# A two-layer block on one core: the first half of x2 is formed during the scan, the work behind the scan is reordered, and the first decay and delta times u go ahead of x's high parts and remainders

## The chip, the core and the metric

The kernel runs on one core of a Trainium2 chip. The core has TensorE (PE), VectorE (DVE), ScalarE (ACT), GpSimd (POOL), SyncE (SP, which issues most transfers) and 16 DMA engines. Each engine works through its own queue in order, and the engines wait for one another on semaphores. The metric is the device time of one execution in microseconds; lower is better.

## The reference, cut to what matters

`x` is (4, 256, 256), `ctx` is (4, 256, 128), so there are 1024 tokens of 256 channels.

```python
x = x + tanh(g_xattn[0]) * attention(layernorm(x), ctx, ...)               # x1
x = x + tanh(g_ffn[0])   * ffn(layernorm(x), w_gate_up, w_proj)            # x2
x = x + tanh(g_xattn[1]) * ssm(ctx, z=layernorm(x), ...)                   # x3
x = x + tanh(g_ffn[1])   * moe(layernorm(x), router, gate, up, down)       # result

# ffn, both weight matrices quantised to three values per group of 64
h = silu(x @ gate.T) * (x @ up.T)
hn = h * rsqrt(mean(h * h) + eps)
return hn @ w_proj.T

# ssm: 16 states n for each of 256 channels e, 256 time steps, 4 batches
state = state * exp(delta * A) + (delta * u) * B
y = sum_over_n(state * C) + D * u
return y * silu(z)

# moe: 64 experts, 8 per token, 128 slots per expert
logits = x @ router; top 8; gather, two matmuls, silu, one matmul, scatter
```

## The kernel before, in words

Every engine has its program written out by hand, one function per engine, and nothing reorders it.

**Up to the scan.** Attention, convolution, `delta`, the quantisation of the feed-forward weights and the normalisation of x1 are done. PE turns the normalised rows into banks 1 to 4 (`transpose_tokens(2, ...)`), one bank per pair of channel half and token half. ACT's `keep_high(k)` (L831) copies bank 1 + k into `x_high` at a shorter mantissa, and DVE (L1543) subtracts that from the bank into `x_low`, the remainder, so that two matmuls stand for one of full precision. ACT's `keep_quantised(k)` (L824) copies the turned ternary weights out of banks 5, 6, 7 and 0. DVE multiplies `delta` by `u` into bank 5 (L1548), once bank 5 has been read.

**The scan.** 64 steps k (4 phases of 16 states; a step covers 512 tokens). Per step ACT's `decay(k)` (L861) writes exp(delta A) into one of three buffers `dA`; DVE's `state(k)` multiplies bank 5 by the row B (L1565, into bank 6 or 4 in turn) and runs the recurrence (L1570) into one of four buffers `hs`. Two steps make one POOL `product` (L612) with C, which PE turns and sums into bank 3 (L1104). A DVE step that reuses a buffer of `hs` waits for the product that read it two pairs before. The step's unit f = k // 4 also carries one of 16 slices of the feed-forward block: PE's `gate_up(f)` (L1162), ACT's silu (L898, with a load of its table before and one back for the exponential), the gate times up on DVE (`hidden`, L1578) or, for every fourth f, on POOL, its square (ACT L881, POOL L626) and PE's `project` (L1135). At f = 8 the projection of the first four token tiles is complete and ACT copies it to `xn` (L874); at f = 10 POOL forms their root of mean squares (`rms(0)`, L631).

**Behind the scan.** DVE forms the last product (L1627), the mean squares of the second half (L1554), coefficient and x2 of tiles 0 to 3 (L1602, L1608), their statistics (L1614, L1617), then the same for tiles 4 to 7, three small tables from `ident` (L1636 to L1639, used far later, by the routing), and y times silu(z) (`gated`, L1645). ACT keeps the last y (`keep_y(3)`, L868), the turned x2 (`keep_x2`, L917) and silu of the normalised x2 (`gate_z`, L923). PE turns x2 (L1206) and y (L1258), and computes the router's logits of x2 (L1225) and of y (L1233). Then come the choice of 8 experts (`select`), the list of slots, and the loop over 64 experts, which ends the program.

## Time and profile before

| | us |
|---|---|
| median of 3 runs (lowest, highest) | 399.18 (398.72, 400.62) |
| the profiled execution, its own time | 399.68 |
| its span, first to last instruction | 397.9 |
| up to the scan | 0 to 62.3 |
| start of the scan and scan | 62.3 to 194.0 |
| behind the scan, up to the second half of the logits | 194.0 to 211.7 |
| choice and slots, up to the first expert's rows | 211.7 to 229.3 |
| expert loop and end | 229.3 to 397.9 |
| PE busy, DVE busy, ACT busy, POOL busy (share of the span) | 328.9 (83%), 303.7 (76%), 257.6 (65%), 247.4 (62%) |

All times in the sections below count from the start of the span. A busy time is that of the engine's own instructions; a row of a timeline gives the start, the length, the engine, the line, what is written from what, and in brackets how long the engine sat idle before it and for whom. The length of a DVE or ACT instruction includes some 0.1 us in which the next one already runs.

### The profile page before, as it was taken

How to read it: one execution, taken by the hardware profiler on the slowest of the kernel's cores; microseconds unless marked ns; L12 is line 12 of the kernel's file. 1: busy time of each engine (PE TensorE's matmuls, PEld its weight loads, DVE VectorE, ACT ScalarE, POOL GpSimd, SP SyncE). 2: the span in 40 equal slices, each digit the busy share in tenths (PEclk: the TensorE clock that was granted, in tenths of full speed). 3: DMA queues.
4: the chain of work that ended last, by engine and by line, in shares of the span. 5: the costliest groups of instructions: out<-in, count | busy, mean ns of one | idle time of the engine just before them, and what ended most of it. 6: DMA issues, size and time to landing. Idle time of an engine off the chain costs nothing.

```text
span 397.9 us, 6795 instructions
## 1 busy us (share of the span) xinstructions
PE 328.9 (83%) x1854; PEld 270.4 (68%) x1857; DVE 303.7 (76%) x669; ACT 257.6 (65%) x528; POOL 247.4 (62%) x194
## 2 busy tenths in 40 slices
PE   3947964887797699598885189999999999999994
PEld 2433643575585578487685177888888888888863
DVE  2999999999999999999999946554544455544485
ACT  1798999998888898888264345445544554445412
POOL 4200025779887778797423488888787888787410
PEclk9996885799999989989999579999999999999999
DMA  8940620776344887341297348888898888874464
GB/s 232 366 155 2 172 80 26 246 265 222 115 151 165 272 259 262 109 158 54 61 263 187 115 108 219 213 216 225 223 225 233 229 223 221 212 156 94 67 189 144
DMA packets 57835, 70.96 MB, mean 178 GB/s; under 512 B 6659, under 2 KB 42163, under 8 KB 57811
## 3 DMA queue, kind: packets, MB, share of 16 engines
q1 hardware_dynamic: 49104, 56.04, 46.0%
q0 software_dynamic: 7536, 14.56, 15.9%
q10 hardware_dynamic: 1170, 0.08, 0.2%
q8 instruction: 11, 0.18, 0.2%
q14 instruction: 14, 0.11, 0.1%
HBM read 61.75 MB, written 8.91 MB: 178 GB/s over the span
## 4 chain that ended last, share of the span: by engine, by line
PE 43%; DVE 15%; ACT 10%; DMA 7%; issue 7%; POOL 1%; DVEq 0%; SPq 0%; POOLq 0%
PE bank L1326 14%; PE bank L1349 11%; PE bank L1319 7%; DVE bank L1565 5%; DMA ssm<-bc_rows 4%; PE bank L1306 4%; DVE ssm L1570 3%; ACT ssm L861 3%; DMA B_last<-bc_rows 2%; ACT L898 2%; PE bank L1312 2%; ACT L861 1%; ACT ffn L898 1%; PE bank L1162 1%; PE bank L1233 1%
## 5 line engine op out<-in xcount | busy, mean ns | idle before, releaser
L612 POOL TENSOR_TENSOR ssm<-ssm,arena 128x1024 f32<-128x1024 f32 x31 | 73.7, 2376 | 19.5 <-DVE ssm L1570 11.4
L683 POOL DMA_INDIRECT ssm<-routed,idx x64 | 67.7, 1058 | 21.8 <-issue 18.6
L1570 DVE TENSOR_TENSOR_SCAN ssm<-ssm,bank 128x512 f32<-128x512 f32 x64 | 78.1, 1221 | 2.2
L1326 PE MATMUL bank<-places,ye_parts 128*128 128x512 f32 x264 | 75.8, 412 | 0.5 <-DVE ye_parts L1782 0.5
L1790 DVE SCALAR_TENSOR_TENSOR ssm<-ssm,bank 128x96 f32<-128x96 f32 x64 | 20.1, 314 | 71.8 <-ACT ssm L970 71.7
L694 POOL DMA_INDIRECT sums<-ssm,idx x31 | 52.9, 1706 | 14.4 <-issue 9.4
L970 ACT ACTIVATE ssm<-bank 128x96 f32<-128x96 f32 x64 | 16.0, 250 | 69.9 <-PE bank L1349 69.9
L1349 PE MATMUL bank<-arena,ssm 128*128 (+1 forms) x256 | 53.3, 330 | 1.1 <-ACT ssm L953 1.1
L1326 PEld LDWEIGHTS bank<-places,ye_parts 128*128 128x128 f32 x264 | 45.3, 189 | 12.1 <-DVE ye_parts L1782 0.9
L1349 PEld LDWEIGHTS bank<-arena,ssm 128*128 128x128 f32 x256 | 45.1, 191 | 7.2 <-issue 1.7
L861 ACT ACTIVATE ssm<-delta,A_sb 128x510 f32<-128x510 f32 x64 | 44.1, 716 | 7.8 <-DVE ssm L1570 7.5
L1104 PE MATMUL bank<-ident,ssm 128*128 128x128 f32 x256 | 34.4, 280 | 16.4 <-ACT bc_buf L868 8.4
L580 POOL TENSOR_TENSOR rstd<-rstd,mhalf 128x4 f32<-128x4 f32 x8 | 9.2, 1154 | 62.0 <-DVE rstd L1414 61.9
L1104 PEld LDWEIGHTS bank<-ident,ssm 128*128 128x128 f32 x256 | 29.5, 144 | 21.2 <-POOL ssm L612 10.1
L1319 PE MATMUL bank<-arena,ssm 96*128 (+1 forms) x128 | 38.7, 384 | 0.5 <-ACT ssm L957 0.5
L1565 DVE TENSOR_TENSOR bank<-bank,ssm 128x512 f32<-128x512 f32 x44 | 29.9, 679 | 0.1
L953 ACT ACTIVATE ssm<-bank 128x256 f32<-128x256 f32 x64 | 24.5, 383 | 7.5 <-PE bank L1306 7.5
L1306 PE MATMUL bank<-ident,ssm 128*128 128x128 f32 x128 | 25.5, 282 | 4.4 <-DMA ssm<-routed,idx 4.4
L963 ACT ACTIVATE ssm<-bank 128x256 f32<-128x256 f32 x64 | 24.6, 384 | 6.5 <-PE bank L1319 3.6
L1774 DVE TENSOR_SCALAR places<-xin,fix 128x1024 fp32r<-128x1024 f16 x33 | 25.7, 780 | 0.5 <-PE bank L1326 0.4
L1306 PEld LDWEIGHTS bank<-ident,ssm 128*128 128x128 f32 x128 | 23.0, 198 | 4.5 <-DMA ssm<-routed,idx 4.4
L1162 PE MATMUL bank<-x_high,w_gate 128*128 128x512 f32 x32 | 16.0, 501 | 8.8 <-ACT w_up L824 3.3
(232 smaller groups left out, 698.4 us busy)
## 6 DMA issues: line engine op xcount, KB each, us to landing
ssm<-bc_rows SPq DMA_DIRECT2D x22, 512.0 KB, 3.8
arena<-bc_rows SPq DMA_DIRECT2D x16, 512.0 KB, 5.0
arena<-in_L_ffn_gate_proj SPq DMA_DIRECT2D x32, 192.0 KB
arena<-in_L_ffn_up_proj SPq DMA_DIRECT2D x32, 192.0 KB
arena<-in_L_ffn_down_proj SPq DMA_DIRECT2D x32, 192.0 KB
B_last<-bc_rows SPq DMA_DIRECT2D x10, 512.0 KB, 3.8
sums<-zero_f SPq DMA_DIRECT2D x1, 2304.0 KB, 14.1
arena<-in_L_ffn_w_gate_up SPq DMA_DIRECT2D x1, 2048.0 KB, 11.4
```

Of the source, the lines that this page charges most:

```text
L612: pool.tensor_tensor(prod[:, a:b, :], hs[:, a:b, :], C_all[:, 2 * (q % 8):2 * (q % 8) + 2, :], ALU.mult).then_inc(s.prod_ok, 1)
L683: pool.indirect_dma_start(out=xe[:, k, :], out_offset=None, in_=routed, in_offset=bass.IndirectOffsetOnAxis(ap=idx2[:, k, 0:1], axis=0)).t ...
L694: pool.indirect_dma_start(out=sums, out_offset=bass.IndirectOffsetOnAxis(ap=idx2[:, k, 1:2], axis=0), in_=ye[:, k, :], in_offset=None, com ...
L861: act.activation(part(dA[:, k % 3, 0:1], (L, 2), (1, L - 1), offset=1), part(delta[:, h, 0:1], (L, 2), (1, L - 1), offset=th * 512 + 1), A ...
L1104: ins = pe.matmul(bank[3][:, t * P:t * P + P], prod[:, a, t * P:t * P + P], ident[:, :], start=first and t == 0, stop=False, is_transpose= ...
L1306: ins = pe.transpose(of_input()[:, t * P:t * P + P], part(xe[:, k, 0:1], (2, P), offset=t), ident[:, :])
L1319: pe.matmul(of_result(), hhT[0:I, k % 2, :], w_dn[:, bass.ds(slot, 1), :], start=True, stop=True).then_inc(s.m_y_ps, 1)
L1326: ins = pe.matmul(bank[4 + 2 * h + t][:, :], ye_parts[:, b, c, h * P:h * P + P], places[:, b, 4 * t:4 * t + 4, :], start=False, stop=False ...
L1349: ins = pe.matmul(bank[1][:, 0:2 * I], xeT[:, k % 2, t * P:t * P + P], w_gu[:, :, bass.ds(slot, 1), t * I:(t + 1) * I], start=t == 0, stop ...
L1565: dve.tensor_tensor(x[:, :], bank[5][:, :], B_buf[q % 3][:, k % 2, :], ALU.mult).then_inc(s.dBu_ok, 1)
L1570: dve.tensor_tensor_scan(hs[:, k % 4, :], dA[:, k % 3, :], x[:, :], 0.0, ALU.mult, ALU.add).then_inc(s.scan_ok, 1)
L1774: dve.tensor_scalar(places[:, b, :, :].rearrange("p j m -> p (j m)"), token, part(fix[:, 0:1], (1, 1), offset=e), None, ALU.is_equal).then ...
```

## The change

It makes five edits.

1. At the scan's start ACT copies the first two weight banks, forms `decay(0)`, copies two of x's high parts (that of bank 4 first, because step 1 writes there), forms `decay(1)`, and copies the other two. DVE multiplies delta by u at once and forms the remainders two by two behind steps 0 and 1. POOL's first half of the second delta waits for `du_ps` instead of for the first remainder.
2. At f = 10 POOL also forms the coefficients of tiles 0 to 3; at f = 12 ACT scales their projection in place (four copies); at f = 13 POOL adds them to the residual in one instruction of 128x1024. DVE no longer does this.
3. DVE takes the mean squares of the second half ahead of the last product, and puts `mean_over_deviation(3, 0)` between the second pair and the third of tiles 4 to 7.
4. PE turns x2's first half ahead of the last sums, and both own parts and turns come in another order; ACT takes `keep_x2(0)` ahead of `keep_y(3)`.
5. The three small tables from `ident` move to the start of the program.

```diff
@@ POOL
-            pool.wait_ge(s.xs_rest, 1)
+            pool.wait_ge(s.du_ps, 1)
             pool.tensor_tensor(Bbc[:, 1, :], du[:, 1, :], Bbc[:, 1, :], ALU.subtract).then_inc(s.delta_second, 1)
             pool.wait_ge(s.delta_second, 1)
-            pool.wait_ge(s.du_ps, 1)
...
                 if f == 10:
                     rms(0)
+                    pool.wait_ge(s.rms_ok, 1)
+                    pool.wait_ge(s.tg_sb, 1)
+                    pool.tensor_tensor(coef[:, 0:4], rinv[:, 0:4], part(tg[:, 2:3], (0, 4)), ALU.mult).then_inc(s.rms_ok, 1)
+                if f == 13:
+                    pool.wait_ge(s.po_copy, 6)
+                    pool.tensor_tensor(x_res[:, 0:4, :], xw[:, 0:4, 0:D], x_res[:, 0:4, :], ALU.add).then_inc(s.x2_sb, 4)
                 product(2 * f + 1)
@@ ACT
-                act.wait_ge(s.q_step, 8)
+                act.wait_ge(s.q_step, 10)
...
-            for k in range(4):
-                keep_high(k)
             keep_quantised(0)
             keep_quantised(1)
...
             decay(0)
+            keep_high(3)
+            keep_high(0)
             decay(1)
+            keep_high(1)
+            keep_high(2)
             keep_quantised(2)
...
+                if f == 12:
+                    act.wait_ge(s.rms_ok, 2)
+                    act.wait_ge(s.po_copy, 2)
+                    for j in range(4):
+                        act.activation(xn[j], xn[j], ACT.Copy, scale=coef[:, j:j + 1]).then_inc(s.po_copy, 1)
...
+            keep_x2(0)
             keep_y(3)
-            keep_x2(0)
@@ PE
-                pe.wait_ge(s.xs_rest, k + 1)
+                pe.wait_ge(s.xs_rest, k + 2)
...
-            sum_early(UNITS - 1)
-            sum_late(UNITS - 1)
...
             turn_x2(0)
+            sum_early(UNITS - 1)
+            sum_late(UNITS - 1)
+            own_part(0)
             turn_y(0)
+            turn_x2(1)
             logits_of_x2(0)
-            turn_x2(1)
-            own_part(0)
             turn_y(1)
@@ DVE
+            dve.wait_ge(s.c_ident, 1)
+            dve.tensor_reduce(d_e[:, :], ident[:, :].rearrange("p (a b) -> p b a", b=GE), AX.X, ALU.add).then_inc(s.diag_ok, 1)
...
-            for k in range(4):
-                kc, c = k % 2, slice((k // 2) * 512, (k // 2) * 512 + 512)
-                dve.wait_ge(s.xs_hi, k + 1)
-                dve.tensor_tensor(x_low[:, kc, c], bank[1 + k][:, :], x_high[:, kc, c], ALU.subtract).then_inc(s.xs_rest, 1)
...
+            def rest(n):
+
+                k = (3, 0, 1, 2)[n]
...
+                if k == 1:
+                    dve.wait_ge(s.xs_rest, 1)
...
                 state(4 * f)
+                if f == 0:
+                    rest(0)
+                    rest(1)
                 state(4 * f + 1)
+                if f == 0:
+                    rest(2)
+                    rest(3)
...
+            mean_squares(1, bank[7])
             dve.tensor_tensor(prod[:, 2:4, :], hs[:, 2:4, :], C_all[:, DS - 2:DS, :], ALU.mult).then_inc(s.last_ok, 1)
-            mean_squares(1, bank[7])
-            coefficient(0, 2)
-            x2(0)
             half_statistics(3, 0, x2_of, s.x2_sb)
-            coefficient(1, 3)
-            x2(1)
+            second_coefficient()
+            x2((4, 5))
             mean_over_deviation(3, 0)
+            x2((6, 7))
             half_statistics(3, 1, x2_of, s.x2_sb)
```

Where the scan starts, DVE's program reads as follows before (`x_low` is the remainder, bank 5 receives delta times u, banks 6 and 4 the input of steps 0 and 1, `ssm` holds the scan's buffers):

```order
L1538 MEMSET ssm 128x6 [waits q_step]
L1543 TENSOR_TENSOR x_low_52<-bank1,x_high_51 128x512 [waits xs_hi]
L1543 TENSOR_TENSOR x_low_52<-bank2,x_high_51 128x512 [waits xs_hi]
L1543 TENSOR_TENSOR x_low_52<-bank3,x_high_51 128x512 [waits xs_hi]
L1543 TENSOR_TENSOR x_low_52<-bank4,x_high_51 128x512 [waits xs_hi]
L1548 TENSOR_TENSOR bank5<-delta,u 128x512 [waits delta_sb,u_sb,quantT_sb]
L1565 TENSOR_TENSOR bank6<-bank5,ssm 128x512 [waits ld_B0,du_ps,quantT_sb]
L1570 SCALAR_TENSOR_TENSOR ssm<-ssm,bank6 128x512 [waits dA_ok,dBu_ok]
L1565 TENSOR_TENSOR bank4<-bank5,ssm 128x512 [waits ld_B0]
L1570 SCALAR_TENSOR_TENSOR ssm<-ssm,bank4 128x512 [waits dA_ok,dBu_ok]
L1565 TENSOR_TENSOR bank6<-bank5,ssm 128x512 [waits scan_ok,ld_B1]
```

and as follows now (the lines are those of the changed file):

```order
L1555 MEMSET ssm 128x6 [waits q_step]
L1560 TENSOR_TENSOR bank5<-delta,u 128x512 [waits delta_sb,u_sb,quantT_sb]
L1586 TENSOR_TENSOR bank6<-bank5,ssm 128x512 [waits ld_B0,du_ps,quantT_sb]
L1591 SCALAR_TENSOR_TENSOR ssm<-ssm,bank6 128x512 [waits dA_ok,dBu_ok]
L1568 TENSOR_TENSOR x_low_52<-bank4,x_high_51 128x512 [waits xs_hi]
L1568 TENSOR_TENSOR x_low_52<-bank1,x_high_51 128x512 [waits xs_hi]
L1586 TENSOR_TENSOR bank4<-bank5,ssm 128x512 [waits xs_rest,ld_B0]
L1591 SCALAR_TENSOR_TENSOR ssm<-ssm,bank4 128x512 [waits dA_ok,dBu_ok]
L1568 TENSOR_TENSOR x_low_52<-bank2,x_high_51 128x512 [waits xs_hi]
L1568 TENSOR_TENSOR x_low_52<-bank3,x_high_51 128x512 [waits xs_hi]
L1586 TENSOR_TENSOR bank6<-bank5,ssm 128x512 [waits scan_ok,ld_B1]
```

The same eleven instructions stand in both; the four remainders have moved from in front of delta times u to behind steps 0 and 1.

Behind the scan, PE's program reads as follows before (L1148 are the squares' sums, L1104 the last sums of y, L1206 the turn of x2, L1258 that of y, L1225 the logits of x2, L1216 the own part):

```order
L1148 MATMUL bank<-ones_f,ffn 128x1 [waits acc_ok]
L1148 MATMUL bank<-ones_f,ffn 128x1 x3
L1104 MATMUL bank<-ident,ssm 128x128 [waits prod_ok]
L1104 MATMUL bank<-ident,ssm 128x128 x7
L1104 MATMUL bank<-ident,ssm 128x128 [waits last_ok]
L1104 MATMUL bank<-ident,ssm 128x128 x7
L1206 MATMUL bank<-ident,x_res 128x128 [waits xn4T_sb,x2_sb,ss_sb,scan_ok]
L1206 MATMUL bank<-ident,x_res 128x128 [waits x2_sb] x7
L1258 MATMUL bank<-ident,bc_buf 128x128 [waits xn4T_sb,y_sb]
L1258 MATMUL bank<-ident,bc_buf 128x128 x7
L1225 MATMUL bank<-router_sb,ssm 128x64 [waits xn4T_sb,x2_sb]
```

and as follows now:

```order
L1160 MATMUL bank<-ones_f,ffn 128x1 [waits acc_ok]
L1160 MATMUL bank<-ones_f,ffn 128x1 x3
L1216 MATMUL bank<-ident,x_res 128x128 [waits xn4T_sb,x2_sb,ss_sb,scan_ok]
L1216 MATMUL bank<-ident,x_res 128x128 [waits x2_sb] x7
L1116 MATMUL bank<-ident,ssm 128x128 [waits prod_ok]
L1116 MATMUL bank<-ident,ssm 128x128 x7
L1116 MATMUL bank<-ident,ssm 128x128 [waits last_ok]
L1116 MATMUL bank<-ident,ssm 128x128 x7
L1226 MATMUL bank<-ident,ssm 128x128 [waits xn4T_sb]
L1226 MATMUL bank<-ident,ssm 128x128 x7
L1268 MATMUL bank<-ident,bc_buf 128x128 [waits xn4T_sb,y_sb]
L1268 MATMUL bank<-ident,bc_buf 128x128 x7
```

The first turn of x2 has moved ahead of the last sums of y, and the own part ahead of the turn of y.

## Rows read from the trace of the kernel before

**Rows 1.** Stretches: start:end, length, busy us of each engine (instructions), TensorE's clock, DMA share, GB/s.

```profile
62.30:67.36 5.06, 3.34 (x22) 2.56 (x21) 4.97 (x9) 5.06 (x10) 2.36 (x1) 0.50 0.00 0
104.00:106.00 2.00, 0.00 (x0) 0.00 (x0) 1.97 (x3) 1.99 (x3) 2.00 (x2) 1.00 0.11 18
108.00:110.00 2.00, 2.00 (x6) 1.52 (x6) 1.97 (x4) 1.94 (x3) 2.00 (x2) 0.50 0.13 42
194.00:205.60 11.60, 9.36 (x75) 8.15 (x75) 10.93 (x37) 5.79 (x12) 3.60 (x4) 1.00 0.78 206
```

**Rows 2.** Timeline of DVE, start of the scan.

```profile
63.49 0.68 DVE L1543 TENSOR_TENSOR x_low<-bank,x_high 128x512 fp32r<-128x512 f32 x1
65.88 1.38 DVE L1548 TENSOR_TENSOR bank<-delta,u 128x512 f32<-128x512 f32 x1
71.07 0.67 DVE L1565 TENSOR_TENSOR bank<-bank,ssm 128x512 f32<-128x512 f32 x1
...
83.45 1.22 DVE L1570 TENSOR_TENSOR_SCAN ssm<-ssm,bank 128x512 f32<-128x512 f32 x1
```

**Rows 3.** Timeline of the other engines there: POOL, ACT, PE.

```profile
64.34 2.36 POOL L593 TENSOR_TENSOR bc_buf<-du,bc_buf 128x1024 f32<-128x1024 f32 x1 [3.72 <-DVE x_low L1543]
...
60.35 2.06 ACT L794 ACTIVATE xw<-x_res,nmr,rstd 128x256 f32<-128x256 f32 x4
64.32 1.94 ACT L824 ACTIVATE w_gate<-bank 128x1024 fp32r<-128x1024 bf16 x2
72.19 1.57 ACT L861 ACTIVATE ssm<-delta,A_sb 128x510 f32<-128x510 f32 x2
82.54 1.33 ACT L861 ACTIVATE ssm<-delta,A_sb 128x510 f32<-128x510 f32 x2
...
69.44 0.77 PE L1162 MATMUL bank<-x_high,w_gate 128*128 128x512 f32 x1 [3.25 <-ACT w_up L824]
72.56 0.63 PE L1162 MATMUL bank<-x_low,w_up 128*128 128x512 f32 x1
```

**Rows 4.** Timeline of ACT, POOL and DVE around the units f = 12 to 14.

```profile
170.96 0.72 ACT L861 ACTIVATE ssm<-delta,A_sb 128x510 f32<-128x510 f32 x1 [0.53 <-DVE ssm L1570]
173.82 0.60 ACT L898 ACTIVATE ffn<-bank 128x512 f32<-128x512 f32 x1 [0.33 <-PE bank L1162]
175.73 1.33 ACT L861 ACTIVATE ssm<-delta,A_sb 128x510 f32<-128x510 f32 x2
...
176.59 2.41 POOL L612 TENSOR_TENSOR ssm<-ssm,arena 128x1024 f32<-128x1024 f32 x1
...
181.37 1.22 DVE L1570 TENSOR_TENSOR_SCAN ssm<-ssm,bank 128x512 f32<-128x512 f32 x1
```

**Rows 5.** Groups of POOL, shapes apart: count, busy us, mean ns, idle before.

```profile
L602 POOL TENSOR_TENSOR du<-delta,u 128x1024 f32<-128x1024 f32 x1 | 2.4, 2360 | 0.0
L666 POOL TENSOR_TENSOR xw<-xw,rasum 128x256 f32<-128x256 f32 x2 | 2.0, 978 | 2.5 <-DVE rasum L1680 2.5
```

**Rows 6.** Timeline behind the scan, all engines.

```profile
192.23 2.34 POOL L612 TENSOR_TENSOR ssm<-ssm,arena 128x1024 f32<-128x1024 f32 x1
194.06 1.58 DVE L1627 TENSOR_TENSOR ssm<-ssm,arena 128x1024 f32<-128x1024 f32 x1
195.80 1.02 POOL L631 TENSOR_TENSOR rinv<-ssum,mhalf 128x4 f32<-128x4 f32 x1 [1.23 <-DVE ssum L1554]
195.89 1.67 DVE L1608 SCALAR_TENSOR_TENSOR x_res<-xw,coef,x_res 128x256 f32<-128x256 f32 x4
202.99 0.39 DVE L1636 TENSOR_REDUCE d_e<-ident 128x8 f32<-128x128 f32 x1
```

**Rows 7.** Chain of work that ended last, behind the scan: start, us, what.

```profile
201.31 2.08 ACT xnT L923 x4
203.39 0.97 ACT ssm L917 x2
204.50 1.07 PE bank L1258 x8
```

More of the change, by code:

```diff
@@ L1435, in mean_over_deviation @@
                 dve.scalar_tensor_tensor(out=nmr[:, t], in0=mv[:, t, 0], scalar=-1.0, in1=rstd[:, t], op0=ALU.mult, op1=ALU.mult).then_inc(s.nmr_ok, 1)
+            dve.wait_ge(s.c_ident, 1)
+            dve.tensor_reduce(d_e[:, :], ident[:, :].rearrange("p (a b) -> p b a", b=GE), AX.X, ALU.add).then_inc(s.diag_ok, 1)
+            dve.tensor_reduce(d_hi[:, :], ident[:, :].rearrange("p (a b) -> p a b", b=GE), AX.X, ALU.add).then_inc(s.diag_ok, 1)
+            dve.wait_ge(s.diag_ok, 2)
+            dve.tensor_copy(d_eh[:, :], d_e[:, :]).then_inc(s.diag_ok, 1)
             for b in range(2):
@@ L1549, in _ @@
             dve.wait_ge(s.quantT_sb, 2)
+            def rest(n):
+                k = (3, 0, 1, 2)[n]
+                kc, c = k % 2, slice((k // 2) * 512, (k // 2) * 512 + 512)
+                dve.wait_ge(s.xs_hi, n + 1)
+                dve.tensor_tensor(x_low[:, kc, c], bank[1 + k][:, :], x_high[:, kc, c], ALU.subtract).then_inc(s.xs_rest, 1)
             def mean_squares(c, src):
@@ L1592, in _, with second_coefficient, x2 @@
                     dve.tensor_tensor(router_sb[:, :, :], router_sb[:, :, :], part(bank[2][:, 0:1], (0, 2), (1, E)), ALU.subtract).then_inc(s.coef_ok, 1)
-            def coefficient(c, n):
-                dve.wait_ge(s.rms_ok, c + 1)
-                if c == 0:
-                    dve.wait_ge(s.po_copy, 2)
-                else:
-                    dve.wait_ge(s.proj_ok, UNITS)
-                dve.tensor_scalar(coef[:, 4 * c:4 * c + 4], rinv[:, 4 * c:4 * c + 4], tg[:, 2:3], None, ALU.mult).then_inc(s.coef_ok, 1)
-                dve.wait_ge(s.coef_ok, n)
-            def x2(c):
-                for j in range(4 * c, 4 * c + 4):
-                    dve.scalar_tensor_tensor(out=x_res[:, j, :], in0=xn[j] if c == 0 else bank[1 + j // 2 - 2][:, (j % 2) * D:(j % 2) * D + D], scalar=coef[:, j:j + 1], in1=x_res[:, j, :], op0=ALU.mult, op1=ALU.add).then_inc(s.x2_sb, 1)
+            def second_coefficient():
+                dve.wait_ge(s.rms_ok, 3)
+                dve.wait_ge(s.proj_ok, UNITS)
+                dve.tensor_scalar(coef[:, 4:8], rinv[:, 4:8], tg[:, 2:3], None, ALU.mult).then_inc(s.coef_ok, 1)
+                dve.wait_ge(s.coef_ok, 2)
+            def x2(tiles):
+                for j in tiles:
+                    dve.scalar_tensor_tensor(out=x_res[:, j, :], in0=bank[1 + j // 2 - 2][:, (j % 2) * D:(j % 2) * D + D], scalar=coef[:, j:j + 1], in1=x_res[:, j, :], op0=ALU.mult, op1=ALU.add).then_inc(s.x2_sb, 1)
             def half_statistics(n, c, source, ready):
@@ L1626, in _ @@
             dve.wait_ge(s.sum_ok, 4 * (UNITS - 1))
+            mean_squares(1, bank[7])
             dve.tensor_tensor(prod[:, 2:4, :], hs[:, 2:4, :], C_all[:, DS - 2:DS, :], ALU.mult).then_inc(s.last_ok, 1)
-            mean_squares(1, bank[7])
-            coefficient(0, 2)
-            x2(0)
             half_statistics(3, 0, x2_of, s.x2_sb)
-            coefficient(1, 3)
-            x2(1)
+            second_coefficient()
+            x2((4, 5))
             mean_over_deviation(3, 0)
+            x2((6, 7))
             half_statistics(3, 1, x2_of, s.x2_sb)
-            dve.tensor_reduce(d_e[:, :], ident[:, :].rearrange("p (a b) -> p b a", b=GE), AX.X, ALU.add).then_inc(s.diag_ok, 1)
-            dve.tensor_reduce(d_hi[:, :], ident[:, :].rearrange("p (a b) -> p a b", b=GE), AX.X, ALU.add).then_inc(s.diag_ok, 1)
-            dve.wait_ge(s.diag_ok, 2)
-            dve.tensor_copy(d_eh[:, :], d_e[:, :]).then_inc(s.diag_ok, 1)
             def gated(c, h):
```

## Prediction

> **What bounds the kernel now.** I read the stretches first. From 62.3 to the end of the scan DVE is the engine without gaps: 4.97 of 5.06 us where the scan starts and 1.97 of 2.00 inside it, whatever PE does there (nothing between 104 and 106) [rows 1]. So inside the scan only two things count: what DVE itself does, and whether another engine becomes late for it. Behind the scan, from 194.0, DVE is busy 10.93 of 11.60 us, PE 9.36 [rows 1], and the chain of waits runs over DVE, then ACT, then PE [rows 6, 7]. The expert loop from 229 on is not touched and only starts earlier or later. The change therefore acts at three places, each read in its own timeline: the start of the scan, units f = 10 to 14, and the stretch behind the scan.
>
> **Start of the scan.** DVE's work there is the same eleven instructions in another order, so only a gap or a length can be gained. One length can: delta times u took 1.38 us for 512 columns [rows 2], while POOL's subtraction ran from 64.34 to 66.70 [rows 3]; it ended at 67.26, 0.56 behind POOL's. Now POOL waits for it, so it runs alone. DVE's last product of 1024 columns likewise ended 1.07 behind POOL's, at 195.64 against 194.57 [rows 6]; 512 columns at that rate are 0.54, and with the 0.1 that a DVE instruction adds I estimate 0.66. The working:
>
> - ACT is free at 62.4, when the four normalised rows end [rows 3], and now begins with the two weight banks, 1.94, to 64.3, then the first decay, 0.72, to 65.0.
> - DVE: delta times u from about 63.6, when the first bank is copied, to 64.3. Step 0 multiplies at 64.4, scans at 65.1. Two remainders follow at 66.2 (0.60 each: the four ran from 63.49 to 65.97 [rows 2]), step 1 at 67.4, 1.85 long, two remainders at 69.3, step 2 at 70.45. It began at 71.07 [rows 2]: 0.6 earlier.
> - ACT does the same work in another order, without a gap (5.06 of 5.06 us [rows 1]), so it can't follow by itself. It is late first at step 8: the decay, first of a pair from 82.54, ends at 83.26, and the scan starts at 83.45 [rows 2, 3], 0.2 of room. ACT gains only the wait that lies in the pair at 72.19: 1.57 against 1.33 for two [rows 3], 0.24. So DVE can be ahead by 0.43 at step 8, not by 0.6.
> - The last remainder now ends at 70.5 instead of 66.0. PE's first gate_up starts then, at 70.9 and not 69.44; it took 3.75 to the end of its last matmul at 73.19 [rows 3], so it ends at 74.65. ACT reaches the first silu, behind the pair at 72.19 and a table load, at 75.06 before and 74.8 now. It is just covered. Without that cover, each tenth is a tenth more for step 8.
>
> This part gives 0.45, between 0.1 (PE later than reckoned) and 0.6.
>
> **Inside the scan.** The added work is not on DVE, and costs nothing while it fits in ACT's and POOL's gaps.
>
> - f = 10: one more POOL instruction of 128x4, at most the 1.02 of the same shape with a power [rows 6]. POOL waits for the scan in that unit; nothing.
> - f = 12: four ACT copies of 128x256 take 2.0, as the four of that shape from 60.35 do [rows 3]. ACT absorbs two waits right behind them, 0.53 and 0.33 [rows 4]; the decay of step 56 moves from 175.73 by 1.1 and ends at 177.55. Its scan starts two steps ahead of that at 181.37 [rows 4], at 177.68. It fits by 0.1.
> - f = 13: POOL's addition of 128x1024. The row of the same size and engine has 2.36; the row with a broadcast operand has 0.98 for 256 columns, so 3.9 for 1024 [rows 5]. One operand here has gaps between its rows but no broadcast, so I take 2.36. It stands ahead of product 27, which began at 176.59 and now ends at 176.59 + 2.36 + 2.41 = 181.36 at the latest. Step 58 reuses that product's buffer and starts at 181.37 [rows 4]. Room is about nothing: I put 0.05 as a stall. At 3.9 the stall is 1.5.
>
> **Behind the scan.** The last product goes on ending where it did: it starts at 194.06, but ends 1.07 behind POOL's product (192.23 + 2.34), at 195.64 [rows 6]. The mean squares, put ahead of it, take place in that wait. Then DVE drops the first coefficient, which filled 195.64 to 195.89, and four x2 of 1.67 together: the statistics begin at 195.6, 1.9 earlier. Up to the first table row at 202.99 [rows 6] DVE then needs 7.10 - 1.67 = 5.43, and 0.2 for `mean_over_deviation`, which now waits for POOL's power: its place is 201.3. The three tables (0.70 in front of `gated`) are gone too, done in DVE's idle time at the start. But the second `mean_over_deviation` now meets POOL's power of 1.02 [rows 6] with nothing to hide it: 201.4 + 1.02 and hand-overs give 202.55; with 0.15 and the second `gated`, 0.75, the logits of y can start at 203.45. Before, PE started them at 205.5, when the turn of y (204.50 + 1.07) was done [rows 7]. That turn waits for ACT: silu of x2, 2.08, then `keep_x2(1)`, 0.97 [rows 7]. Now silu begins at 198.8 (POOL's power ends at 198.55), so these end at 201.95 and PE's turn at 203.1: not late. PE's last sums and the turn of y come 0.4 later than before, at 197.1 and 198.9, far ahead of `gated` at 201.3. So the logits come 1.9 to 2.05 earlier, and the last `gated`, for which silu starts at 202.7, 1.85 earlier. I take 1.9, bounds 1.6 to 2.1. All behind it keeps its order; the experts' first weights were issued behind the last product, which moves by the scan's gain alone, and are not waited for.
>
> **Sum.** 0.45 - 0.05 + 1.9 = 2.3 us. Against the profiled execution's 399.68 that is 397.4. That execution stands 0.5 above the median of 399.18, for which I forecast **396.9**; its own range, from the terms' bounds without the stall of 1.5, is 396.5 to 397.4. About 0.5% (2.0 us) is what a measurement of this kernel tells from no change, so the forecast stands just beyond it.
>
> **Rivals.**
>
> - *The scan starts no sooner for good.* If PE's first gate_up or step 8's decay gives back the 0.45, only 1.9 is left: 397.3. For it: room of 0.1 to 0.2 at both places. Against: ACT's waits further on show room again. Chance 0.10.
> - *POOL becomes the bound at f = 13.* At 3.9 for the addition DVE stalls 1.5: 398.4. For it: no room by the sum above. Against: POOL's product with the same number of columns takes 2.4. Chance 0.09.
> - *POOL's second power takes its place ahead of DVE's last product.* Both are ready when product 30 ends at 194.57. If the power of 1.02 went first and held the product up, 1.0 is lost: 397.9. Against: four two-operand instructions of DVE at 195.89 ran in 1.67 beside the power at 195.80 [rows 6] and were not held up. Chance 0.05. The Trainium skill ("SBUF — State Buffer", section "Who interferes with whom") says that a DVE instruction with two SBUF inputs and a GpSimd instruction that reads SBUF contend, and the second to start waits for the whole of the first. By that rule the sum would be 1.3 instead of 2.3. The long rows agree with it (1.38 for delta times u), the short one at 195.80 does not.
> - *The tail waits for something else*, y or a transfer, and the change doesn't do what it says there: 0.45 is left, 398.7. Against: every other chain above ends more than 2 us ahead. Chance 0.07.
> - *Slower: TensorE's clock falls behind the scan.* The rows show a fall to 0.50, its level of 1.2 GHz, at 108 to 110, behind a stretch in which PE did nothing [rows 1]. Behind the scan it had 1.00, 2.4 GHz, with PE busy 9.36 of 11.60. POOL's later product 27 leaves PE idle a little longer near 180, and the new order makes PE wait for ACT. Each us at the lower level costs up to 0.5, so it decides from some 4.6 us on; the whole 9.36 at half speed would end 7.1 later than now and give 405.9 with the scan's gain. Against: the longest idle time that I reckon for PE behind the scan is 0.6. Chance 0.05.
>
> **How the numbers follow.** The forecast has the remaining 0.64. The range takes in its bounds, the runs' own spread of 0.5 below, and the first three rivals, up to 398.4; the last two, 0.12 together, are left out: 396.0 to 398.5. Faster by over 0.5% (below 397.2) is the greater part of the forecast's own range: 0.55. Within 0.5%: the other 0.09 and the four rivals with 0.10, 0.09, 0.05 and 0.07, together 0.40. Slower by over 0.5%: 0.05.
>
> **What would show it.** Delta times u at 0.7 instead of 1.38, step 2's first instruction near 70.5, and no idle time of DVE longer than 0.2 in front of step 8, 56 or 58. POOL's addition near 2.4. The last scan's end 0.4 earlier (193.5). The first statistics behind the last product within 0.1 of its end, and the logits of y near 203.0 in the new trace (203.45 less the scan's gain). It is wrong if DVE shows an idle time of over 0.5 in the scan, if the logits wait for the turn of y, or if the clock in 194 to 206 is below 1.00.

## The result, and the profile after

The changed kernel takes **397.5 us** (median of 6 runs, 396.37 to 397.62) against 399.57 for the kernel before in the same session (median of 6, 398.72 to 400.68): a ratio of 0.9945, 95% interval 0.9929 to 0.9962. Its profiled execution has a span of 395.8 us, against 397.9. The forecast was 396.9, range 396.0 to 398.5.

To see where the 2.1 us between the spans come from, I cut both traces at rows that both have: ACT's first normalised row in front of the scan, the scan of step 8, the last scan, the first row of the choice of experts for the first token half (`select`), that for the second half, and the end. The numbers are differences of starts of rows; the experiments' are put beside them here and taken up one by one below.

| kernel | ACT's row to step 8 | step 8 to last scan | last scan to first choice | first to second choice | second choice to end | lowest clock of a whole us, 190 to 200 |
|---|---|---|---|---|---|---|
| before | 23.10 | 109.30 | 14.63 | 4.36 | 186.16 | 1.00 |
| changed | 22.69 | 109.30 | 12.74 | 4.28 | 186.23 | 1.00 |
| E1, edit 1 alone | 22.69 | 109.31 | 14.61 | 4.36 | 185.60 | 1.00 |
| E2, edits 2 to 5 | 23.10 | 109.30 | 12.74 | 4.27 | 186.17 | 1.00 |
| E3, without edit 4 | 22.68 | 109.30 | 12.72 | 4.28 | 185.77 | 1.00 |
| E4, without edit 2 | 22.69 | 109.31 | 16.30 | 4.40 | 185.57 | 0.50 |
| E5, without 2 and 4 | 22.69 | 109.30 | 14.59 | 4.28 | 185.81 | 0.50 |
| E6, edit 2 alone | 23.09 | 109.31 | 13.65 | 4.40 | 187.20 | 0.50 |
| E7, gating first | 22.67 | 109.30 | 13.10 | 4.39 | 185.35 | 0.50 |
| E8, two additions | 22.70 | 111.72 | 12.73 | 4.27 | 186.40 | 1.00 |
| E9, PE filled | 22.67 | 109.30 | 12.74 | 4.28 | 185.72 | 1.00 |
| E10, one wait | 22.80 | 109.31 | 14.62 | 4.35 | 185.27 | 1.00 |
| E11, E6 with PE filled | 23.10 | 109.31 | 12.77 | 4.35 | 186.18 | 1.00 |
| E12, E7 with PE filled | 22.70 | 109.30 | 12.83 | 3.66 | 185.79 | 1.00 |

The change gains 0.41 at the scan's start, neither gains nor loses inside the scan, and gains 1.89 up to the first choice and 0.08 more up to the second: 2.38 in all. The profiled execution of the changed kernel reached ACT's row 0.21 later (60.56 against 60.35) and took 0.07 longer at the end, which leaves 2.1. Those two are no part of the change's effect that these traces can show: that row starts anywhere from 60.02 to 61.38 over all fourteen profiles, and the stretch from the second choice to the end differs by up to 1.9. That difference lies in the expert loop: from the second choice to the loop's first gather it takes 14.44 to 14.46 in all fourteen, from there to the end 170.8 to 172.8. E5, E8, E10 and E11 were executed once each, so what is said of them rests on their traces.

**Start of the scan.** The timeline of the changed kernel there, rows of DVE, POOL and ACT:

```profile
63.91 0.70 DVE L1560 TENSOR_TENSOR bank<-delta,u 128x512 f32<-128x512 f32 x1
64.78 2.35 POOL L593 TENSOR_TENSOR bc_buf<-du,bc_buf 128x1024 f32<-128x1024 f32 x1 [3.94 <-DVE bank L1560]
...
70.79 0.69 DVE L1586 TENSOR_TENSOR bank<-bank,ssm 128x512 f32<-128x512 f32 x1
...
72.33 1.33 ACT L864 ACTIVATE ssm<-delta,A_sb 128x510 f32<-128x510 f32 x2
...
74.97 0.60 ACT L905 ACTIVATE ffn<-bank 128x512 f32<-128x512 f32 x1
...
82.44 1.34 ACT L864 ACTIVATE ssm<-delta,A_sb 128x510 f32<-128x510 f32 x2
...
83.25 1.22 DVE L1591 TENSOR_TENSOR_SCAN ssm<-ssm,bank 128x512 f32<-128x512 f32 x1
```

Delta times u takes 0.70 instead of 1.38 [rows 2], since POOL's subtraction now starts behind it. Step 2 starts at 70.79, against 71.07 before [rows 2], in an execution that is 0.21 late: 0.49 sooner. The wait of 0.24 in ACT's pair at 72.19 [rows 3] is gone (1.33 now), and its first silu (74.97) follows its table load without a wait for PE, whose first gate_up is done at 74.36 (its last matmul starts at 73.97 and takes 0.39). Of the lead of 0.49, 0.41 is left at step 8, as ACT's decay of that step (first of the pair at 82.44) ends just ahead of its scan at 83.25.

**Units f = 12 to 14.** The timeline of the same kernel:

```profile
169.52 1.69 ACT L924 ACTIVATE xw<-xw,coef 128x256 f32<-128x256 f32 x4
...
176.26 2.40 POOL L645 TENSOR_TENSOR x_res<-xw,x_res 128x1024 f32<-128x1024 f32 x1
...
178.63 4.67 POOL L611 TENSOR_TENSOR ssm<-ssm,arena 128x1024 f32<-128x1024 f32 x2
...
181.17 1.22 DVE L1591 TENSOR_TENSOR_SCAN ssm<-ssm,bank 128x512 f32<-128x512 f32 x1
```

ACT's four copies take 1.69, POOL's addition 2.40. The first of the two products at 178.63 ends near 180.97 (half of 4.67), and the scan that waits for it starts at 181.17 without idle time: 0.2 of room.

**Behind the scan.** DVE's rows of the kernel before that the stretches are cut at (last scan, first statistics, first choice):

```profile
192.75 1.22 DVE L1570 TENSOR_TENSOR_SCAN ssm<-ssm,bank 128x512 f32<-128x512 f32 x1
...
197.48 1.40 DVE L1614 BATCH_NORM_STATS2 stats<-x_res 128x6 f32<-128x256 f32 x4
...
207.38 0.62 DVE L1660 MAX8 top<-bank 128x8 f32<-128x64 f32 x4
```

The timeline of the changed kernel, all engines but SP:

```profile
192.55 1.22 DVE L1591 TENSOR_TENSOR_SCAN ssm<-ssm,bank 128x512 f32<-128x512 f32 x1
...
193.95 1.51 DVE L1652 TENSOR_TENSOR ssm<-ssm,arena 128x1024 f32<-128x1024 f32 x1
...
194.13 1.06 PE L1216 MATMUL bank<-ident,x_res 128*128 128x128 f32 x8 [0.95 <-DVE ssm L1591]
194.34 2.01 POOL L630 TENSOR_TENSOR rinv<-ssum,mhalf 128x4 f32<-128x4 f32 x1
...
195.03 1.91 PE L1116 MATMUL bank<-ident,ssm 128*128 128x128 f32 x16
195.39 1.39 DVE L1638 BATCH_NORM_STATS2 stats<-x_res 128x6 f32<-128x256 f32 x4
...
198.58 2.08 ACT L935 ACTIVATE xnT<-x_res,nmr,rstd 128x256 f32<-128x256 f32 x4 [1.00 <-DVE nmr L1447]
...
202.25 0.16 DVE L1447 SCALAR_TENSOR_TENSOR nmr<-mv,rstd 128x4 f32<-128x4 f32 x1 [0.46 <-POOL rstd L580]
202.33 0.75 DVE L1665 SCALAR_TENSOR_TENSOR u<-bank,tg,xnT 128x512 f32<-128x512 f32 x1
...
205.29 0.61 DVE L1680 MAX8 top<-bank 128x8 f32<-128x64 f32 x4
...
209.57 0.62 DVE L1680 MAX8 top<-bank 128x8 f32<-128x64 f32 x4 [0.53 <-PE bank L1243]
```

The chain of waits of the same kernel (start, us, what):

```profile
201.21 1.02 POOL rstd L580
...
202.33 0.76 DVE u L1665
...
203.13 2.00 PE bank L1243 x16
205.13 0.88 PE bank L1251 x8
206.01 1.73 PE bank L1235 x16
207.75 1.80 PE bank L1243 x16
```

`mean_over_deviation(3, 0)` stands between x2 of tiles 5 and 6 (at 198.38). The statistics start right behind the last product: 2.84 behind the last scan's start (192.55), against 4.73 before (197.48 and 192.75). The chain goes over POOL's power and the second gating to PE's logits of y at 203.13 (it was ACT's silu and the turn of y [rows 7]), and from there to the second choice PE works without a gap. Two stretches of it, columns as in [rows 1], show the clock at 1.00 and PE busy 11.45 of 12.00, more than the 9.36 of 11.60 of before [rows 1]:

```profile
194.00:200.00 6.00, 5.75 (x49) 5.30 (x50) 5.86 (x20) 3.10 (x6) 3.35 (x3) 1.00 0.52 143
...
200.00:206.00 6.00, 5.70 (x52) 5.46 (x51) 4.71 (x18) 4.98 (x9) 1.01 (x1) 1.00 1.11 262
```

### The profile page after: what moved, and what is told of

The parts are those of the page before. It is cut to its first block, busy times and chain, and to the rows that moved or that the text cites. A ratio compares the mean times of both kernels' runs of the same rounds, so it can differ in the third digit from the quotient of the medians.

```text
span 395.8 us, 6802 instructions
## 1 busy us (share of the span) xinstructions
PE 327.5 (83%) x1857; PEld 269.8 (68%) x1857; DVE 301.5 (76%) x664; ACT 259.0 (65%) x532; POOL 251.2 (63%) x196
## 4 chain that ended last, share of the span: by engine, by line
PE 43%; DVE 24%; ACT 15%; DMA 9%; issue 7%; POOL 1%; DVEq 0%; SPq 0%; POOLq 0%
PE bank L1338 14%; PE bank L1361 11%; PE bank L1331 7%; DVE bank L1586 5%; DMA ssm<-bc_rows 4%; PE bank L1318 4%; DMA B_last<-bc_rows 3%; ACT ssm L864 3%; DVE ssm L1591 3%; ACT L905 2%; DVE u L1478 2%; PE bank L1324 2%; DVE q_sum L1484 2%; PE bank L1025 1%; ACT L864 1%
## 5 line engine op out<-in xcount | busy, mean ns | idle before, releaser
L625 POOL TENSOR_TENSOR ffn<-ffn 128x512 f32<-128x512 f32 x16 | 20.4, 1273 | 2.7 <-ACT ffn L884 2.7
```

## The experiments

My theory was that two independent gains add up: 0.4 at the scan's start, and 1.9 behind the scan from taking x2's first half off DVE. The rivals gave the second gain to the new order of PE, or to the moved tables.

### E1 and E2: each place alone

E1 is the kernel before with edit 1, E2 the changed kernel with edit 1 undone. Edit 1, cut to DVE's part (E1 has it, E2 does not):

```diff
-            for k in range(4):
...
-                dve.tensor_tensor(x_low[:, kc, c], bank[1 + k][:, :], x_high[:, kc, c], ALU.subtract).then_inc(s.xs_rest, 1)
...
                 state(4 * f)
+                if f == 0:
+                    rest(0)
+                    rest(1)
```

> The kernel before with edit 1 alone (the order at the scan's start). My theory: two gains that add up, and this is the small one. Delta times u takes 0.7 us instead of 1.38, step 2 begins 0.5 to 0.6 us sooner after it, ACT's decay of step 8 caps the lead at 0.4, and the scan ends 0.4 sooner; the time is 0.3 to 0.5 us under that of before (0.999 of it). The rival that the scan starts no sooner for good expects the end of the scan within 0.1 of before and no gain. A rival that puts the whole change on the start expects more than 1 us.

> The changed kernel with edit 1 undone (edits 2 to 5 alone). My theory: the scan starts and ends as before, the logits of y come 1.9 to 2.0 us sooner after the scan's end, and the time is 1.5 to 2.0 us under that of before; with e1's gain it adds up to that of the whole change, within 0.3 us. The rival that POOL has no room at f = 13 expects an idle time of DVE of over 0.3 us near step 58 here, where the scan is not ahead. The rival that the edits hang on one another expects a sum that misses by more than 0.5 us.

E1 gained 0.41 at the start and nothing elsewhere; its time is 0.9989 of before (0.9975 to 1.0003), which fits 0.4 us but by itself can't be told from no change. E2 gained 1.89 and 0.09 behind the scan and nothing at the start; 0.9969 (0.9946 to 0.9991), 1.2 us with an interval of 0.4 to 2.2. In both the scan between takes 109.30 to 109.31, and DVE shows one idle time in it, 0.85 in front of the last gate times up, as before. So in the traces the two gains are independent and add up (the timed runs do not contradict it, but are too wide to show the sum), and POOL is not late at f = 13 even where the scan is not ahead.

### E3 to E5: the order of PE, and what it hangs on

E3 undoes edit 4 in the changed kernel, E4 edit 2, E5 both. Edit 4 undone, cut to PE's first part:

```diff
             squares(1, bank[7])
+            sum_early(UNITS - 1)
+            sum_late(UNITS - 1)
...
             turn_x2(0)
-            sum_early(UNITS - 1)
-            sum_late(UNITS - 1)
-            own_part(0)
             turn_y(0)
```

Edit 2 undone, cut to DVE's part:

```diff
             dve.tensor_tensor(prod[:, 2:4, :], ...)
+            coefficient(0, 2)
+            x2(0, range(4))
             half_statistics(3, 0, x2_of, s.x2_sb)
```

> The changed kernel with edit 4 undone (PE and ACT in the old order behind the scan). My theory: DVE sets the end of that stretch, so the order of PE is worth little: ACT keeps the turned x2 later, silu of tiles 0 to 3 starts 0.5 to 0.7 us later, and the logits of y start 0.4 to 0.5 us later; 0.3 to 0.6 us of time lost against the changed kernel. The rival that the tail's gain comes from PE's order expects 1.5 us or more lost, with DVE idle in front of the gating; the rival that PE's order is covered altogether expects 0.1 or less.

> The changed kernel with edit 2 undone (coefficient and x2 of tiles 0 to 3 on DVE again, behind the last product). My theory: these five instructions (1.67 us and some 0.15) stand on the path again: the first statistics start 1.8 to 1.9 us later behind the product, the logits of y 1.6 to 1.9 us later, the time is 1.5 to 1.9 us over the changed kernel's. The rival that the gain comes from the order or from the moved tables expects 0.8 us or less. POOL's power, held to 2.01 us by the last product in the changed kernel, stays so here, since it stands at the same place.

> The changed kernel with edits 2 and 4 undone. From the last scan to the first choice of experts (L1680's first row) the kernel before takes 14.63 us, the changed one 12.74, and e4, without edit 2, took 16.30. My theory after e4: edit 4's order lets PE wait for x2's first half, which without edit 2 is late, with the last sums of y queued behind and the clock falling to 0.50; with the old order PE does the sums of y in that time, so this stretch takes 14.4 to 14.7 us and the clock stays at 1.00. The rival that the excess of e4 comes from another part (the mean squares ahead, the moved `mean_over_deviation`) expects 16 us or more again.

**E3** lost nothing in its trace: 12.72 us to the first choice. My 0.4 to 0.5 was wrong there, and the rival that PE's order is covered was right. Its timeline:

```profile
194.00 2.17 PE L1116 MATMUL bank<-ident,ssm 128*128 128x128 f32 x16 [1.25 <-POOL ssm L611]
196.02 1.04 PE L1218 MATMUL bank<-ident,x_res 128*128 128x128 f32 x8
...
198.14 2.08 ACT L935 ACTIVATE xnT<-x_res,nmr,rstd 128x256 f32<-128x256 f32 x4 [0.35 <-DVE nmr L1447]
```

The last sums of y begin as soon as POOL's product is there and end at 196.2, 4.0 behind the last scan's start (192.13). So PE has turned x2 and ACT has kept it before `nmr` comes, and silu starts 6.01 behind the last scan, against 6.03 in the changed kernel: it waits for DVE either way. The timed runs say less: the ratio is 0.9968 (0.9949 to 0.9986), which overlaps that of the changed kernel, but the profile is of one of E3's faster runs (397.35), the median of its 12 is 398.81, and seven of them (398.59 to 399.76) are longer than any of the changed kernel's six. What those seven met, and whether edit 4 makes it rarer, is not shown.

**E4** lost 3.6 us against the changed kernel, twice what I expected, and is slower than the kernel before: 400.63, a ratio of 1.0021 (1.0006 to 1.0035). PE's rows of its timeline:

```profile
196.44 2.42 PE L1205 MATMUL bank<-ident,x_res 128*128 128x128 f32 x8 [3.08 <-DVE x_res L1624]
...
198.65 3.34 PE L1105 MATMUL bank<-ident,ssm 128*128 128x128 f32 x16
```

A stretch of it behind the scan, columns as in [rows 1]:

```profile
196.40:200.00 3.60, 3.56 (x15) 3.02 (x16) 3.53 (x15) 1.20 (x2) 0.75 (x2) 0.50 0.76 217
```

PE's queue now has x2's first turn ahead of the last sums of y. With x2 on DVE again, PE waits 3.08 us for it, the sums and all of y stand behind that wait, and the granted clock falls to 0.50, so that sixteen sums take 3.34 and not 1.91. **E5**, with the old order too, comes to 14.59, where the theory said 14.4 to 14.7, although its clock, which the theory had at 1.00, fell as well (0.50 from 194 to 197). So of the 3.6 us, 1.85 are edit 2's own (14.59 less 12.74) and 1.7 are the price of edit 4's order where x2 is late, with the longer fall of the clock in it (about 7 us in E4, 3 in E5), which these two runs can't divide from it. Edit 4 gains nothing in the traces and is safe only together with edit 2. Edits 3 and 5, all that E5 has behind the scan beside the kernel before, come to 0.04 with the clock down.

### E6 and E11: edit 2 alone, without and with the clock up

E6 is the kernel before with edit 2. E11 adds nine turns (transpositions) of the identity matrix into a bank that nobody reads, where PE waits for POOL's last product.

```diff
             squares(1, bank[7])
+            for k in range(9):
+                pe.transpose(bank[0][:, (k % 4) * P:(k % 4) * P + P], ident[:, :], ident[:, :])
```

> The kernel before with edit 2 alone. My theory: this edit carries the tail's whole gain; the first statistics start 1.83 us sooner behind the last scan, everything behind follows, and from the last scan to the first choice it takes 12.8 us (14.63 before, 12.74 with all edits); the start of the scan is as before. The rival that the order of PE, the moved mean squares or the moved tables carry a part of it expects 13.2 us or more.

> The kernel before with edit 2 alone and nine turns of the identity in PE's idle time behind the scan. e6, without them, took 13.65 us from the last scan to the first choice, with the clock at 0.50 from 194.5 to 197.5. My theory: 0.65 us of that is the clock's, which put PE's first turn of x2's second half behind ACT; with the clock up it takes 12.95 to 13.1, so edit 2 alone is worth 1.5 to 1.7 of the 1.89 and the other edits behind the scan 0.2 to 0.35. The rival that the clock does nothing there expects 13.5 or more; the rival that edit 2 carries all expects 12.8.

E6's timeline:

```profile
194.73 3.50 PE L1115 MATMUL bank<-ident,ssm 128*128 128x128 f32 x16 [1.25 <-POOL ssm L612]
...
195.91 1.02 POOL L631 TENSOR_TENSOR rinv<-ssum,mhalf 128x4 f32<-128x4 f32 x1 [1.23 <-DVE ssum L1565]
...
202.43 1.09 ACT L928 ACTIVATE ssm<-bank 128x512 f32<-128x512 f32 x2 [0.65 <-PE bank L1217]
...
204.59 0.75 DVE L1652 SCALAR_TENSOR_TENSOR u<-bank,tg,xnT 128x512 f32<-128x512 f32 x1 [1.19 <-ACT xnT L934]
```

A stretch of E6, columns as in [rows 1]:

```profile
194.50:197.50 3.00, 2.77 (x13) 2.77 (x14) 2.97 (x11) 0.00 (x0) 1.20 (x2) 0.50 0.14 31
```

E11's timeline:

```profile
194.47 2.18 PE L1115 MATMUL bank<-ident,ssm 128*128 128x128 f32 x16 [0.21 <-POOL ssm L612]
...
203.72 0.75 DVE L1654 SCALAR_TENSOR_TENSOR u<-bank,tg,xnT 128x512 f32<-128x512 f32 x1 [0.57 <-ACT xnT L934]
```

The same stretch of E11:

```profile
194.50:197.50 3.00, 3.00 (x26) 2.72 (x26) 2.97 (x12) 0.82 (x2) 1.08 (x2) 1.00 0.26 67
```

E6 came to 13.65 and spoke against the theory, but its clock was at 0.50: the sums took 3.50, ACT waited 0.65 for PE's turn of x2's second half, and DVE 1.19 for ACT. E11, with the clock at 1.00, takes 12.77. So **edit 2 alone carries 1.86 of the 1.89**, and I had expected only 1.5 to 1.7 of it; the fall of the clock costs 0.88 in this stretch, not 0.65. That 0.88 is one pair of profiles. (E6's timed ratio is 0.9974, 0.9956 to 0.9991, beside 0.9969 for E2.)

### E7, E9 and E12: PE's idle time, and an order that is better still

In the changed kernel DVE waits 0.46 for POOL's power with the second gating behind it. E7 exchanges the two; E9 fills PE's idle time of 0.95 in front of x2's turn with seven turns of the identity (as in E11) and leaves the rest; E12 does both.

```diff
             gated(0, 0)
-            mean_over_deviation(3, 1)
             gated(0, 1)
+            mean_over_deviation(3, 1)
```

> The changed kernel with the second gating of the first token half ahead of the second `mean_over_deviation`, whose wait for POOL's power (0.46 us) held it up. My theory: the logits of y start when the turn of y is done, 0.3 us sooner; silu of the second half and the first choice come 0.2 us later, which the wait of 0.53 in front of the second choice absorbs; the second choice and the end come 0.3 us sooner. The rival that silu of the second half bounds that stretch expects the second choice 0.1 to 0.2 us later.

> The changed kernel with seven turns of the identity into a bank that nobody reads (7 times 0.13 us) in PE's idle time of 0.95 us in front of the first turn of x2. In the profiles so far that idle time is the same whether the granted clock then falls to 0.50 (e4 to e7) or stays at 1.00 (e1 to e3). My theory: the idle time is what lets the clock fall in some executions; filled, it stays at 1.00 from 190 to 204, the stretch from the last scan to the first choice takes 12.7 to 12.8 us as in the changed kernel's profile, and the runs lie closer together than those of e2 and e3 (396.2 to 402.1), with a median at or under 397.5. The rival that the clock's fall has another cause, or comes from the load up to then, expects it in some of these executions too: a spread of runs as before.

> e7 (the second gating ahead of the second `mean_over_deviation`) with the seven turns of e9. In e7 the clock was at 0.50 from 195 to 198, so what its edit is worth stayed open. My theory: with the clock up the logits of y start 0.3 us sooner than in e9, the first choice 0.0 to 0.2 us later, and the second choice 0.2 to 0.3 us sooner, from the last scan to the second choice 16.75 instead of 17.0. The rival that silu of the second half bounds it expects 17.1 to 17.2.

A stretch of E7:

```profile
195.00:198.00 3.00, 3.00 (x16) 3.00 (x15) 2.93 (x12) 1.19 (x2) 2.00 (x2) 0.50 0.39 115
```

The same stretch of E12:

```profile
195.00:198.00 3.00, 3.00 (x30) 2.95 (x29) 2.93 (x13) 1.35 (x3) 2.00 (x2) 1.00 0.46 136
```

E12's timeline at the gating:

```profile
200.89 1.41 DVE L1667 SCALAR_TENSOR_TENSOR u<-bank,tg,xnT 128x512 f32<-128x512 f32 x2
...
202.22 0.16 DVE L1449 SCALAR_TENSOR_TENSOR nmr<-mv,rstd 128x4 f32<-128x4 f32 x1
...
202.52 1.90 PE L1245 MATMUL bank<-router_sb,u 128*128 128x64 f32 x16
```

E7 alone decided nothing: PE's clock was at 0.50 from 195 to 198, and from the last scan to the second choice it took 17.49 (its time is 397.21, a ratio of 0.995, 0.9934 to 0.9965). With the clock up, E12 takes 16.49, against 17.02 in E9 and in the changed kernel: the logits of y start 10.10 behind the last scan instead of 10.59, and the second choice comes 0.53 sooner, where I had expected 0.2 to 0.3. Silu of the second half starts 0.1 later and does not matter. This is also where edits 3 and 5 show their use: with them silu of the first half starts 6.03 behind the last scan, in E11 without them 6.70, but the changed order spends that lead on the wait for POOL's power, which the three tables fill in E11. E12's time is 396.79 (0.9929 of before, 0.9908 to 0.9949), the lowest of all; its interval overlaps that of the changed kernel, so the 0.53 rests on the trace.

E9 has the changed kernel's stretches to 0.02 and its time (397.47; 0.9944, 0.9922 to 0.9966), so filling by itself gains nothing when the clock is up anyway. Its 6 runs lie between 396.69 and 398.51, closer than the 12 of E2 (396.95 to 402.13) and of E3 (396.18 to 399.76), and not closer than those of the changed kernel. In the three profiles with PE filled the clock stayed at 1.00; in those without, it fell in E4 to E7 and stayed up behind the scan in the other seven, with idle times of 0.95 to 1.25 in E3, E5, E6 and E7 alike. That agrees with the idle time letting the clock fall, by chance, but three profiles don't show that the filling prevents it.

### E8: POOL's room at f = 13

```diff
                     pool.wait_ge(s.po_copy, 6)
+                    pool.tensor_tensor(xw[:, 4:8, 0:D], xw[:, 0:4, 0:D], x_res[:, 0:4, :], ALU.add).then_inc(s.po_copy, 1)
+                    pool.wait_ge(s.po_copy, 7)
```

> The changed kernel with POOL's addition of 128x1024 made twice at f = 13 (once into rows that are free). My theory: room at that place is about nothing (step 58's scan starts 0.2 us behind the product that it waits for), so the second addition, 2.4 us, makes DVE wait 2.1 to 2.4 us in front of step 58's scan, the rest of the scan moves by as much and none of it comes back. The rival that POOL has room there expects a wait of under 0.5 us; the rival that the loss is made up by the end of the scan expects the scan's end less than 1 us later.

Its timeline of POOL and DVE:

```profile
177.07 2.41 POOL L645 TENSOR_TENSOR xw<-xw,x_res 128x1024 f32<-128x1024 f32 x1
...
179.63 2.36 POOL L647 TENSOR_TENSOR x_res<-xw,x_res 128x1024 f32<-128x1024 f32 x1
...
181.94 4.67 POOL L611 TENSOR_TENSOR ssm<-ssm,arena 128x1024 f32<-128x1024 f32 x2
...
184.42 1.22 DVE L1593 TENSOR_TENSOR_SCAN ssm<-ssm,bank 128x512 f32<-128x512 f32 x1 [2.45 <-POOL ssm L611]
```

DVE waits 2.45 in front of step 58's scan, and the scan takes 2.42 longer (111.72 against 109.30): none of it comes back. The wait is just above the 2.1 to 2.4 of the theory, and the theory holds: there was room for one addition and for 0.1 to 0.2 more.

### E10: the start's gain by one wait

```diff
-            pool.wait_ge(s.xs_rest, 1)
+            pool.wait_ge(s.du_ps, 1)
             pool.tensor_tensor(Bbc[:, 1, :], du[:, 1, :], Bbc[:, 1, :], ALU.subtract).then_inc(s.delta_second, 1)
             pool.wait_ge(s.delta_second, 1)
-            pool.wait_ge(s.du_ps, 1)
```

> The kernel before with one wait changed: POOL's first half of the second delta waits for delta times u instead of the first remainder, so DVE's delta times u runs with POOL idle; the order of DVE and ACT stays. My theory: the gain at the start is that instruction's length, so this alone takes 0.68 us out (0.70 instead of 1.38), step 2 begins 0.6 to 0.7 us sooner, ACT's wait of 0.24 goes, and step 8's scan starts 0.40 sooner, 22.7 us behind ACT's first normalised row as in the changed kernel (23.10 before). The rival that the reorder carries the gain expects 23.0 to 23.1; the rival that POOL, 1.5 us later than in the changed kernel, becomes late expects an idle time of DVE in front of steps 4 to 8.

Its timeline, DVE, POOL and ACT:

```profile
65.89 0.69 DVE L1547 TENSOR_TENSOR bank<-delta,u 128x512 f32<-128x512 f32 x1
...
66.75 2.35 POOL L593 TENSOR_TENSOR bc_buf<-du,bc_buf 128x1024 f32<-128x1024 f32 x1 [6.12 <-DVE bank L1547]
...
82.34 1.34 ACT L860 ACTIVATE ssm<-delta,A_sb 128x510 f32<-128x510 f32 x2
...
83.15 1.22 DVE L1569 TENSOR_TENSOR_SCAN ssm<-ssm,bank 128x512 f32<-128x512 f32 x1 [0.42 <-DVE bank L1564]
```

Delta times u takes 0.69 here too, and step 2 starts 0.69 sooner (70.38 against 71.07). At step 8 only 0.30 of that is left (22.80): DVE has 0.42 of idle time there, and what it must wait for, though the row names DVE itself, is ACT's decay, first of the pair at 82.34: at 0.72 each [rows 4] it ends at 83.06, 0.09 ahead of the scan, as in the changed kernel (83.16 and 83.25). It is not a late POOL, the third rival: the product whose buffer step 8 reuses starts at 77.98, takes 2.36 and has long been done. So the length of one instruction is 0.30 of the 0.41, by one changed wait, and the reorder adds 0.11, because ACT's order lets its decays come 0.11 sooner.

## Why the prediction was right

- **The forecast.** 2.3 us was predicted, 2.07 measured by medians and 2.38 by the stretches; the time is 0.6 above the forecast and inside the range. The base was 399.18, the median of three runs, and the median of all six of the kernel before is 399.57: 0.4 of the 0.6. The upper end of the forecast's own range is 397.5 by its terms (399.18 - 0.1 - 1.6, with or without the 0.05), not 397.4, and the measured 397.5 lies on it.
- **Start, 0.45.** Measured 0.41. Delta times u, put at 0.66 (its two terms, 0.54 and 0.1, make 0.64), was 0.70; step 2 gained 0.49 rather than 0.6; step 8's decay caps the lead, as said. PE's first gate_up, "just covered" in the text by 0.15, was covered by 0.6: its last matmuls took 0.39 to 0.49 instead of 0.63, as the granted clock rose from 0.50 to 1.00 between 73 and 74. That was not foreseen, and not needed: at the reckoned 3.75 from its start at 71.13 it would have ended at 74.88. E10 shows the step that the text left undecided: most of it is that instruction's length, and a lead of 0.69 on DVE is worth 0.30 if ACT does not come along.
- **Scan, 0.05 lost.** Measured 0. The copies took 1.69 (2.0 reckoned), the addition 2.40 (2.36), and product 27 ended at 180.97 in place of 181.36: room of 0.2. E8 shows that the rival of a late POOL was a real one, and that the next 2.4 us on POOL cost 2.42. The clock of PE near 108 had been 0.50 [rows 1] and was 1.00 in the changed kernel's profile, and the scan took 109.30 in both, so PE's clock there doesn't count.
- **Behind the scan, 1.9.** Measured 1.89 to the first choice, 1.97 to the second; the logits of y, put at 203.0, start at 203.13. The text had the mean squares in a free place, the statistics 1.9 sooner, the new wait for POOL's power and PE's turn not late, and all four are in the rows. E11 shows that its one reason, DVE's dropped instructions, was enough: edits 3, 4 and 5 add 0.03 to the first choice and 0.10 to the second.
- **Wrong: POOL's second power.** The third rival was dismissed with the four x2 instructions that ran beside a power unhurt [rows 6]. In the changed kernel the two did meet, but it was POOL that was held: its power of 128x4 took 2.01, from 194.34 to 0.89 behind the product's end at 195.46, while DVE's product took 1.51 (1.58 before). In E6 the same power behind the product took 1.02, as before [rows 6]. It is 2.00 to 2.01 in all nine profiles with the mean squares ahead of the product, E4 among them as expected, and 1.02 in the other five. The Trainium skill ("SBUF — State Buffer", section "Who interferes with whom") says that a DVE instruction with two SBUF inputs contends with a GpSimd instruction that reads SBUF, that what they share is an exclusive lock, and that issue order decides which of them waits. These rows agree: DVE's product was first. The four x2 beside the power at 195.80 [rows 6], where neither was held, remain unexplained. The power is wanted at 197.18 and is done at 196.35, so it cost nothing.
- **Wrong: PE behind the scan.** The fifth rival took 0.6 for PE's longest idle time and the fall of the clock for an all or nothing of 7 us. The idle time in front of x2's turn is 0.95, and was 1.25 before. The clock did fall in four of the experiments, for 3 to 7 us, and where the pair can be compared it cost 0.88 (E6 against E11) and 1.0 (E7 against E12): enough to halve the gain, not to reverse it. So the rival's chance of 0.05 was too low for a fall and its price too high, and that the clock stayed up in the changed kernel's profile was luck as far as these runs tell. E4 is the way in which the new order could have lost: 3.6 us against the changed kernel and 1.7 against the kernel before, had x2 been late.

What stays open: why the clock falls in one profile and not in another with the same idle time, and so how often the changed kernel's runs meet it; what the longer half of E3's runs met; and what makes the stretches ahead of the scan and in the expert loop differ by up to 1.4 and 1.9 us from profile to profile.

## What to carry to other kernels

Behind a loop that one engine bounds, look first for that engine's work which depends only on things known earlier, and move it into other engines' gaps inside the loop; then count the room of those engines step by step, as the first microsecond may be free and the next full price. An engine's own lead is worth only what the engine that feeds it can follow. Reordering an in-order queue around an operand that has become early gained nothing in the traces here and ties the two edits together: undo the one that makes the operand early, and the other costs more than it ever gave.

## What the runs showed of the hardware

- A POOL power of 128x4 that started while a DVE product of 128x1024 with two operands in SBUF was running ended 0.9 behind that product's end: it took 2.00 to 2.01 us in nine profiles, and 1.02 in the five in which it started behind the product.
- DVE's delta times u, 128x512 with two operands in SBUF, took 1.38 us when it started during a POOL subtraction of 128x1024 and 0.69 to 0.70 with POOL idle (E10 and the changed kernel).
- With the same sixteen sums behind the same idle time of PE (1.25 us) the granted clock stayed at 1.00, 2.4 GHz, before and in E1, E3 and E10, and fell to 0.50, 1.2 GHz, in E5 and E6. Sixteen sums then took 3.48 to 3.50 us instead of 2.17 to 2.18.
- One profile is one draw of this: E6 and E7 read alone would have given the wrong verdict on their edits.
